# Expert stages of a two-block transformer: the row transposes move from behind the gate/up products to behind the activation transposes

## What is computed

```python
logits = router(x)                                  # 8 experts, the 2 best are kept
xs_order = choices_flat.argsort()                   # tokens sorted by expert
sorted_xs = x_flat[xs_indices, :]                   # 4096 tokens x 2 choices
gate_out = ragged_dot(sorted_xs, w_gate, group_sizes=tokens_per_expert)
activation = gelu(gate_out[:, 0, :]) * gate_out[:, 1, :]
expert_outputs = ragged_dot(activation, linear, group_sizes=tokens_per_expert)
out = sum over the 2 choices of expert_outputs[xs_reverse_argsort] * weight
x = x + 0.5 * out                                   # twice in the program, before and after the attention
```

## Time and profile before

| quantity | value |
|---|---|
| median of 3 runs | 4794.32 us (4790.81 to 4796.29) |
| the profiled execution's own time | 4795.79 us |
| its span in the profile | 4794.2 us |
| mean granted TensorE clock | 0.974 |
| PE busy over the span | 4591.8 us (96%) |
| PEld busy | 3481.9 us (73%) |
| DVE, ACT, POOL busy | 2894.5, 2107.9, 2257.8 us |
| instructions on PE | 27966 |

### The profile page before, as it was taken

One profiled execution on the slowest core, in us unless ns is written; L12 is line 12 of the kernel. 1 busy time (PEld: TensorE's weight loads), 2 busy tenths in 40 slices (PEclk: granted clock), 3 DMA queues, 4 the chain that ended last, 5 costly groups with the idle time before them and its releaser, 6 DMA issues. The chain is left out here.

```text
span 4794.2 us, 82831 instructions
## 1 busy us (share of the span) xinstructions
PE 4591.8 (96%) x27966; PEld 3481.9 (73%) x27967; DVE 2894.5 (60%) x5285; ACT 2107.9 (44%) x4111; POOL 2257.8 (47%) x1724
## 2 busy tenths in 40 slices
PE   6999996999999999999998699999899999999999
PEld 4788885666666666666666578888788877778888
DVE  7222225799999999999974722333455548754444
ACT  4222223466676676676672422222322335433222
POOL 0545433278888888888881054643111007500000
PEclk8999998899999999999999799999999999999999
DMA  7223326757777777777764734433422112250110
GB/s 219 86 94 98 94 83 225 252 109 146 146 146 147 145 147 147 145 147 149 149 138 151 228 100 128 130 122 111 176 71 69 57 51 82 71 198 27 36 36 27
DMA packets 245975, 585.69 MB, mean 122 GB/s; under 512 B 30816, under 2 KB 85088, under 8 KB 221152
## 3 DMA queue, kind: packets, MB, share of 16 engines
q0 software_dynamic: 62064, 317.23, 29.3%
q1 hardware_dynamic: 183536, 263.86, 16.8%
HBM read 263.27 MB, written 121.63 MB: 80 GB/s over the span
## 5 line engine op out<-in xcount | busy, mean ns | idle before, releaser
L1373 POOL TENSOR_TENSOR attend_pairs<-attend_pt 128x1024 f32<-128x1024 f32 x512 | 1259.4, 2483 | 193.1 <-ACT attend_pt L1338 192.6
L1386 DVE TENSOR_REDUCE attend_mx<-attend_am_ps 128x1 f32<-128x512 f32 x2048 | 1251.6, 680 | 124.6 <-PE attend_am_ps L1246 121.2
L1338 ACT ACTIVATE attend_pt<-attend_sc_ps 128x512 f32<-128x512 f32 x2048 | 1040.1, 617 | 283.8 <-PE attend_sc_ps L1234 283.7
L1246 PE MATMUL attend_am_ps<-attention_kst,attend_qst 96*128 96x512 f32 x2048 | 859.2, 425 | 9.1 <-DMA attend_qst<-q_parts 9.0
L1234 PE MATMUL attend_sc_ps<-attend_qst,attention_kst 98*128 98x512 f32 x2048 | 816.5, 400 | 1.5 <-ACT attend_pt L1338 1.3
L1637 PE MATMUL ffn_gu_ps<-ffn_y_hi,ffn_w 128*128 128x512 f32 (+1 forms) x1584 | 566.1, 367 | 3.1 <-DVE ffn_y_lo L1767 3.0
L1246 PEld LDWEIGHTS attend_am_ps<-attention_kst,attend_qst 96*128 96x128 f32 x2048 | 392.9, 192 | 239.0 <-DVE attend_mx L1386 122.8
L1637 PE MATMUL ffn_gu_ps<-ffn_y_lo,ffn_w 128*128 128x512 f32 (+1 forms) x1584 | 565.4, 366 | 0.0
L1260 PE MATMUL attend_pv_ps<-attend_pt,attention_v 128*32 128x256 f32 x8192 | 493.6, 381 | 0.0
L741 DVE TENSOR_TENSOR expert_ac<-expert_gu_ps,expert_gl 128x512 f32<-128x512 f32 x142 | 98.2, 692 | 627.1 <-ACT expert_gl L698 603.4
L1234 PEld LDWEIGHTS attend_sc_ps<-attend_qst,attention_kst 98*128 98x128 f32 x2048 | 389.6, 191 | 87.8 <-ACT attend_pt L1338 11.7
(11 more groups left out here) (329 smaller groups left out, 7721.3 us busy)
## 6 DMA issues: line engine op xcount, KB each, us to landing
attend_pairs<-attend_pairs POOLq DMA_DIRECT2D x189, 1024.0 KB
weights_raw<-experts_dram POOLq DMA_DIRECT2D x76, 512.0 KB
ys<-expert_ob SPq DMA_DIRECT2D x142, 256.0 KB
attend_qst<-q_parts SPq DMA_DIRECT2D x192, 128.0 KB, 4.0
yn<-route_yb SPq DMA_DIRECT2D x64, 256.0 KB
ffn_xb<-x SPq DMA_DIRECT2D x64, 256.0 KB, 2.8
keyvalue_xb<-x SPq DMA_DIRECT2D x64, 256.0 KB, 2.8
weights_lo<-experts_dram SPq DMA_DIRECT2D x24, 512.0 KB, 10.8
```

What stands on the lines that cost most here:

```text
L1246: pe.matmul(am[:, bank, :], qst[0:KROWS, n % 2, h * HALF + hd, :], kst[0:KROWS, o:o + 4 * P], start=True, stop=True).then_inc(am_rdy, 1)
L1338: act.activation(pt[:, u % RING, g * 4 * P:(g + 1) * 4 * P], sc[:, s % SBANKS, :], ACT.Exp, scale=HD ** -0.5).then_inc(p_rdy, 1)
L1373: pool.tensor_tensor(pairs[:, slot(half, j), :], pt[:, 2 * p % RING, :], pt[:, (2 * p + 1) % RING, :], ALU.add).then_inc(pair_rdy, 1)
L1386: dve.tensor_reduce(mx[:, hh, block:block + 1], am[:, am_slot["max", a] % MBANKS, :], AX.X, ALU.max).then_inc(mx_rdy, 1)
```

## The change

In `step` of the PE program `turn_rows(j + 1)` goes directly behind `turn_act(j - 1)`, ahead of `up(j)`, where it stood between `up(j)` and `down(j - 1)`. At the stage's start `turn_rows(1)` goes ahead of `up(0)`. ACT and DVE get the same order: `x_part(j + 1)` ahead of `gelu(j)` and `gate(j)`. Both expert stages change, nothing else does; no operation is added or removed.

```diff
@@ PE
             turn_rows(0, 0, 0)
+            turn_rows(1, 1, 0)
             up(0, 0)
-            turn_rows(1, 1, 0)
 
             def step(j, m, i):
 
                 turn_act(j - 1, 1 - m % 2)
+                turn_rows(j + 1, (m + 1) % AHEAD, i + (m + 1) // AHEAD)
                 up(j, m % 2)
-                turn_rows(j + 1, (m + 1) % AHEAD, i + (m + 1) // AHEAD)
                 down(j - 1, 1 - m % 2)
...
@@ ACT
                     a_part(j - 1, k)
+                    x_part(j + 1, k)
                     gelu(j, 1 - k)
-                    x_part(j + 1, k)
                     out(j - 1, k, i)
...
```

More of the change, by code:

```diff
@@ L709, in _ @@
             x_part(0, 0)
+            x_part(1, 1)
             gelu(0, 0)
-            x_part(1, 1)
             with act.Fori(0, NTL // 2 - 1) as i:
@@ L723, in _ @@
             a_part(j - 2, 0)
+            x_part(j, 0)
             gelu(j - 1, 1)
-            x_part(j, 0)
             out(j - 2, 0, NTL // 2 - 1)
```

## The result

The changed kernel takes 4893.78 us (median of 5 runs, 4882.63 to 4897.32), the kernel before 4796.29 us beside it (5 runs, 4790.81 to 4805.17): a ratio of 1.0192 [1.0178, 1.0207], 97.5 us slower. The forecast was 4890 us. The profiled execution of after took 4897.32 us, with a span of 4895.8 us and a mean granted clock of 0.965 (0.974 before).

The account below looks back on a forecast made before the run. The prediction took PE's instruction stream to bound both expert loops; 14 + 54 + 7 + 21 = 96 us on the profiled 4795.8 made 4892, and 4890 us with the runs' median 1.5 lower, range 4830 to 4930.

Parts of the forecast that it names:

- PE's stream stops, at the gate and at the gather: In both expert loops, a wait for gate or gathered rows holds PE's instruction stream, so `up`'s head is read only afterwards.
- Rival B: At the gather wait, only the transposes are held and `up`'s head is read meanwhile: 4832 us, chance 0.14.
- Gathers behind refills, +54 us: Six refills per stage: the gather behind each lands too late, stopping PE 4.2 us (stage one) or 4.8 us (stage two).
- Rival D: On POOL, the refill starts earlier by as much as the rows do, so no stops: 4810 us, chance 0.05.
- The clock, +21 us: Behind 13 stops, PE's granted clock falls to 0.50, costing 1.6 us each; bounds 0 and 43 us.
- Rival C: Behind the stops, PE's clock falls twice a stop: 21 us more, 4911 us, chance 0.13.
- Stage starts, +7 us: Tile 4's late gather costs 5 us in stage one; `up(0)` behind tile 1's rows costs 1 us in each stage.
- The stream behind the gate, +14 us: Between gate and `up`'s head, `turn_rows`' control instructions and transposes delay PE by 0.55 us a round; bounds 0 and 21 us.
- Fewer switches, 0: On PE, eight transposes in a run save nothing over two groups of four; gain bounded at 14 us, taken as 0.
- Rival E: On PE, the switch costs a hidden 0.1 us and stream and gathers have slack: faster, 4780 us, chance 0.04.

Follow-up runs that it names:

- before_split_first: Kernel before with PE's order unchanged, but on ACT and DVE the next rows' split ahead of gelu and gate: 4933.2 us, ratio 1.0279.

## Why the prediction was right, point by point

**PE's stream stops, at the gate and at the gather.** Right. The table read at 420.3 stands with the transposes that waited for the gather, not with the gate at 416.2, and in `before_split_first`, with a gate 1.03 us later, a step was 0.97 us longer. Rival B, in which only the transposes wait, would have shown table reads at 416.3 and no idle time between transposes and gate/up. In the Trainium skill, Advanced Engine Details and Errata, section "Sequencer Loop", instructions wait in a queue while others are read; neither wait here agrees with that.

**Gathers behind refills, +54 us.** Right. The six steps of stage one took 13.11, 13.11, 13.10, 12.99, 12.94 and 12.90 us, those of stage two 14.29, 14.12, 13.89, 13.42, 13.40 and 13.41 us, against 9.22 us of ordinary ones (near their median; the mean is 9.25): 3.8 and 4.5 us each (forecast 4.2 and 4.8), 50 us together. The refill moved forward by 0.95 - 0.27 = 0.68 us, forecast 0.8; the gather of refill 4 landed 39.7 us behind the down product, forecast 39.9; the head behind it took 1.9 us, forecast 2.2, which is most of what the forecast has too much. Rival D, a refill that moves as far as the rows do, is gone by the 6.1 us that POOL waited for its down product.

**The clock, +21 us.** The mechanism is right, the size too small: 25 us behind the twelve stops, 27 with tile 4's. Behind each of the twelve the next step is 1.5 to 2.95 us longer than 9.22 (10.77 here). The prediction took one stretch at the low level for each stop, as at 422.0. In eight of the twelve the clock stayed at 0.50 for 6.8 us, and was there 0.7 us or more ahead of the first gate/up product. One of them, with its first product at 590.18 (columns as in rows 1):

```profile
589.30:596.10 6.80, 5.92 (x14) 4.67 (x15) 0.69 (x1) 0.25 (x1) 3.26 (x5) 0.50 0.39 111
```

Rival C, the clock falling twice a stop, thus came in part: these eight cost 2.4 us each in the mean, the other four 1.5. Its price, twice the 21 us, did not come; part of such a stretch falls into time in which PE makes no product anyway. The Trainium skill says in TensorE: Matmul & The Clock Gate, section "HAM oscillation — how this bites in real kernels", that recurring waits for transfers put the clock down each time; the trace agrees, with 0.50 behind the stop at 422.0 and a slow run of gate/up products behind each of the other eleven, 6.8 us and more from first to last instead of 5.3.

**Stage starts, +7 us.** Right in sum only, since its parts differ. Tile 4's step in stage one took 12.89 us, 3.7 us more (forecast 5), and the one behind it 1.6 us more by the clock. PE's timeline there:

```profile
150.70 0.60 PE L645 MATMUL expert_at_ps<-all_ident,expert_ac 128*128 128x128 f32 x4
153.41 0.66 PE L620 MATMUL expert_tr_ps<-all_ident,expert_xb 128*128 128x128 f32 x4 [2.12 <-DMA expert_xb<-yn,expert_rows]
155.31 0.84 PE L635 MATMUL expert_gu_ps<-weights_hi,expert_x_hi 128*128 x2 [1.24 <-issue]
```

In stage two, which I had left out, the same step took 10.43 us, 1.2 us more, and stage one's second step 10.77 us, 1.6 us more than before, with the clock at 0.50 for 3.4 us of it. These three make 6.5 us, but only the first stood in the forecast, with 5. That each stage's first product comes 1 us later could not be seen: what lies ahead of it varies by more (122.3 us after, 124.2 before).

**The stream behind the gate, +14 us.** The mechanism is right, the size is not: it measures 25 us, 29 with what the kernel before paid already. The prediction gave control instructions 0.1 us each and took the transposes of rows as almost free, 0.02 us. In the profile after, the four steps of a round have their first gate/up load 0.34, 0.11, 0.20 and 0.10 us later than the transposes' loads would have it, 0.75 us a round in stage one and 0.88 in stage two; before it was 0.08. So it rose by 0.67 and 0.80, where I had 0.55. Two of the four steps show in PEld's timeline:

```profile
478.70 0.47 PEld L620 LDWEIGHTS expert_tr_ps<-all_ident,expert_xb 128*128 128x128 f32 x4
479.25 0.32 PEld L635 LDWEIGHTS expert_gu_ps<-weights_hi,expert_x_hi 128*128 128x128 f32 x2
...
487.86 0.47 PEld L620 LDWEIGHTS expert_tr_ps<-all_ident,expert_xb 128*128 128x128 f32 x4
488.64 0.32 PEld L635 LDWEIGHTS expert_gu_ps<-weights_hi,expert_x_hi 128*128 128x128 f32 x2 [0.31 <-issue]
```

From load to load it is 0.55 us in the first and 0.78 in the second. 0.44 is what the loads of these four transposes take when nothing is late: in the version with early reads they start at 469.00 and the gate/up load at 469.44. 15 rounds by 0.75 and 15 by 0.88 are 24 us. Of the 29 us, 6 lie in the first two steps of the stages: 11.02 and 10.66, 11.53 and 10.87 us with six buffers, 9.58 and 9.07, 10.37 and 9.07 with the early reads as well.

**Fewer switches, 0.** Wrong, it gives 12 to 13 us. The working took the 0.67 us in rows 2 as exactly four transposes and a product. It skipped the line between them, the first down product:

```profile
414.12 0.48 PE L656 MATMUL expert_dn_ps<-weights_hi,expert_a_hi 128*128 x1
```

So four transposes took 0.35 us here (413.77 to 414.12) and the first product 0.32, not 0.23. In rows 2 the 11 down products behind it take 414.44 to 416.98, 0.231 us each; in the version with early reads 12 directly behind gate/up products take 465.95 to 468.67, 0.227 each. The first product gives 0.09 us, the other eleven 0.05, the gate/up products 0.04 (408.19 to 413.77 against 460.41 to 465.95); against that the first of two groups of transposes in a run takes 0.44 instead of 0.35. Left is 9.15 - 9.05 = 0.10 us a step, and 134 steps make 13 us. It was within the bound of 14 that was put down, but the value taken was the lower end, by that misread 0.67. Rival E had this gain right, 4780 us, and the version without both costs runs at 4781. But its other condition, slack in stream and gathers, was not met in the change itself, so nothing shows that 0.04 was too low for it.

**The sum.** These last two errors, +11 and -12, cancel, and so 96 forecast against 97.5 measured is partly luck. So do the stops, 4 us too many, and the clock, 6 too few. In the trace the 93.8 us of the loops are 50 (stops), 25 (clock behind them), 8 (starts, with tile 4 and the clock behind it) and, over the ordinary steps, 9.25 instead of 9.16 us, 12 us in 134 steps. They make 95.

**What stays open.** Why the first products behind a run of transposes come at 0.231 us and not 0.227. It isn't ACT's or DVE's order: in the kernel with PE's new and their old order the down products keep 0.227 (467.96 to 470.45 for eleven). Nor did I find why a gather's landing behind the refill varies between 39.6 and 41.0 us behind the down product's end; that it meets a store of SP was seen but not tried.

## What to carry to other kernels

Before a consumer moves forward, look for the work that its producer's queue does in the meantime: here a refill of 34 us (380.82 to 415.20) stands between two gathers on POOL, and four buffers were just enough, by 1.7 us in the transfers of rows 8, so asking for the rows one `up` earlier cost 12 stops. If an engine waits on a semaphore, count what its instruction stream must still read before the next long work: table reads belong ahead of the wait, and a stop costs that head again as well as the clock behind it. A regrouping with a small gain of its own (0.10 us a step here) should be run together with more buffers (two here) and early reads before it is judged.

## What the runs showed of the hardware that was not expected

Products of one shape had two paces: 0.231 us for down products behind transposes, 0.227 us for the same directly behind other products, and 0.32 us for the very first behind transposes.

A weight load that waits for another engine held up the reading of everything behind it in PE's stream, down to table reads that need nothing from it, while the products queued ahead of it ran on: 0.97 us a step for a gate 1.03 us later. Read ahead of that wait, the two table reads cost nothing that shows (steps of 9.05 us); behind it the head with them took 1.9 us (transposes 420.29, product 422.21) and without them 0.76 us (252.42 to 253.18, at the clock's lower level).

And a stop of 3.9 us cost 5.4 us, because the clock's lower level behind it took another 1.5 us; over the twelve stops this was 1.5 to 2.95 us, and the lower level lasted 3.4 or 6.8 us.
